# Perceiver block: x1 projected raw with column-centred weights, the inverse deviation applied afterwards

## What is computed

```
x = x + xattn(ctx, layernorm(x))          # scores, softmax over the 128 queries, context-weighted sum
x = x + attn(layernorm(x), w_attn, ...)   # 16 heads of 16, causal, T = 128
x = x + ffn(layernorm(x), W, b, V_r, C)   # W plus a rank-32 correction
layernorm(x) = (x - mean) / sqrt(var + 1e-5)
```

## Time and profile before

| what | value |
|---|---|
| median of 3 runs | 105.95 us (105.73 to 106.05) |
| the profiled execution | 105.76 us, of which the span of the instructions is 103.7 us |
| PE busy | 98.3 us of 103.7 |
| DVE, ACT, POOL busy | 76.3, 72.7, 63.8 us |
| read from memory | 27.59 MB |
| context loop, last weighing matmul | starts at 83.79 us |

### The profile page before, as it was taken

The page is one execution under the profiler, slowest core; times in us unless marked ns, Lnnn a source line. Parts: engine busy times, 40 slices in busy tenths (PEclk is TensorE's granted clock), DMA queues, the critical chain, the costliest instruction groups (busy, mean ns, idle before and its releaser), DMA issues.

```text
span 103.7 us, 2257 instructions
## 1 busy us (share of the span) xinstructions
PE 98.3 (95%) x740; PEld 86.4 (83%) x740; DVE 76.3 (74%) x217; ACT 72.7 (70%) x268; POOL 63.8 (62%) x46
## 2 busy tenths in 40 slices
PE   5999999999999999999999999999999999969990
PEld 1389999999999999999999999999998976845660
DVE  0412959959999999988777797777889745699641
ACT  4019599599999999997777977778879304489410
POOL 6405499869999999999766797666886001004020
PEclk9999999999999999999999999999999999999999
DMA  3899999999999999999999999993000000000001
GB/s 70 330 417 412 411 411 406 408 408 408 414 400 409 403 416 406 408 409 409 408 406 406 411 408 409 388 369 125 0 0 6 0 0 0 0 0 0 6 0 51
DMA packets 8746, 27.86 MB, mean 269 GB/s; under 512 B 1120, under 2 KB 1824, under 8 KB 8736
## 3 DMA queue, kind: packets, MB, share of 16 engines
q1 hardware_dynamic: 8736, 27.73, 68.3%
HBM read 27.59 MB, written 0.13 MB: 267 GB/s over the span
## 4 chain that ended last, share of the span: by engine, by line
PE 89%; DVE 4%; DMA 2%; issue 1%; POOL 1%; ACT 0%; DVEq 0%
PE bank L323 43%; PE bank L335 21%; PE bank L338 10%; DVE head_max L716 2%; DMA x<-x_dram 2%; PE bank L406 2%; PE bank L443 1%; PE bank L344 1%; PE bank L419 1%; PE bank L500 1%; PE bank L308 1%; PE bank L486 1%; PE bank L389 1%; PE bank L386 1%; PE bank L462 1%
## 5 line engine op out<-in xcount | busy, mean ns | idle before, releaser
L288 POOL TENSOR_TENSOR rows_split<-rows_ring,rows_split 128x1024 fp32r<-128x1024 f32 (+1 forms) x25 | 58.4, 2335 | 16.9 <-ACT rows_split L518 16.8
L323 PE MATMUL bank<-query_t,cols_ring 128*128 128x128 f32 x392 | 47.5, 276 | 0.0
L323 PEld LDWEIGHTS bank<-query_t,cols_ring 128*128 128x128 f32 x392 | 45.7, 192 | 1.3 <-ACT query_t L509 0.3
L529 ACT ACTIVATE bank<-bank,neg_max 128x128 f32<-128x128 f32 x98 | 33.1, 338 | 7.4 <-DVE neg_max L653 7.2
L335 PE MATMUL bank<-rows_split,probs 128*128 128x512 f32 x92 | 34.7, 413 | 0.0
L518 ACT CAST rows_split<-rows_ring 128x1024 fp32r<-128x1024 f32 (+1 forms) x25 | 25.8, 1033 | 6.1 <-DMA rows_ring<-ctx_rows_dram 5.1
L670 DVE SCALAR_TENSOR_TENSOR probs<-bank,inv_sums,probs 128x128 fp32r<-128x128 f32 x98 | 27.6, 345 | 0.9
L338 PE MATMUL bank<-rows_split,probs 128*128 128x256 f32 x92 | 25.6, 279 | 0.0
L653 DVE TENSOR_REDUCE neg_max<-bank 128x4 f32<-128x512 f32 (+1 forms) x25 | 16.8, 672 | 8.6 <-PE bank L323 8.6
L335 PEld LDWEIGHTS bank<-rows_split,probs 128*128 128x128 f32 x92 | 17.3, 189 | 3.1
L529 ACT ACTIVATION_READ_ACCUMULATOR bank<-bank,neg_max 128x1 f32 x98 | 19.8, 202 | 0.0
(11 more groups left out here) (96 smaller groups left out, 64.0 us busy)
## 6 DMA issues: line engine op xcount, KB each, us to landing
cols_ring<-ctx_cols_dram SPq DMA_DIRECT2D x24, 512.0 KB, 14.8
rows_ring<-ctx_rows_dram SPq DMA_DIRECT2D x24, 512.0 KB, 15.2
wqk_sb<-w_qk_dram SPq DMA_DIRECT2D x1, 512.0 KB, 11.6
cols_ring<-ctx_cols_dram SPq DMA_DIRECT2D x1, 256.0 KB, 11.3
rows_ring<-ctx_rows_dram SPq DMA_DIRECT2D x1, 256.0 KB, 12.1
wv_sb<-w_v_dram SPq DMA_DIRECT2D x1, 256.0 KB, 11.7
wproj_sb<-w_proj_dram SPq DMA_DIRECT2D x1, 256.0 KB, 10.4
wffn_sb<-w_ffn_dram SPq DMA_DIRECT2D x1, 256.0 KB, 9.7
```

The source lines that it names most:

```text
L288: pool.tensor_tensor(rows_split[:, b, 0:n, 1, :], rows_ring[:, slot * STEP:slot * STEP + n, :], rows_split[:, b, 0:n, 0, :].bitcast(F32), ...
L323: last = pe.matmul(into[:, t * P:(t + 1) * P], cols_ring[:, slot * STEP + t, c, :], query_t[:, c, :], start=(c == 0), stop=(c == DC - 1))
L529: last = act.activation(on[:, t * P:(t + 1) * P], on[:, t * P:(t + 1) * P], ACT.Exp, bias=neg_max[:, b, t:t + 1], accum_out=sums[:, b, t:t ...
```

## The change

1. A third copy of the q, k and v weights, turned (`w_t`, 768 KB), is loaded. Its load and those of `w_qk` (512 KB) and `w_v` (256 KB) are issued in the context loop, behind the rows of three steps (`WT_AT` = 13: in the iterations s = 13, 15, 17).
2. DVE sums it along its free axis in three parts at the ends of its steps 14, 15 and 16, and scales the 128 x 6 sums to negative means at its step 17.
3. SP stores those 768 means to memory, element by element (4 bytes each), behind the loads of the last rows; waits until they have landed; loads them back broadcast to all partitions (384 KB); and then issues the eight other weight loads.
4. POOL adds the means to the weights in six parts of 128 x 256: two in its loop behind the row splits of steps 20 and 21, four behind the loop.
5. x1 is turned raw and projected; DVE multiplies the identity by rstd, PE spreads that over all partitions with a matrix of ones, ACT copies the raw projections, DVE multiplies each by the spread rstd, and ACT, POOL and DVE add biases. The values take rstd in `scalar_tensor_tensor`, four instructions in place of two.
6. x1_bias moves from DVE to POOL. The rank-32 correction is no longer summed with the feed-forward weight on PE but by POOL (128 x 512).

```diff
+                if s == WT_AT:
+                    sp.dma_start(wt_sb[:], w_t).then_inc(wt_landed, 16)
+                if s == WT_AT + 2:
+                    sp.dma_start(wqk_sb[:], w_qk).then_inc(wqkv_landed, 16)
+                if s == WT_AT + 4:
+                    sp.dma_start(wv_sb[:], w_v).then_inc(wqkv_landed, 16)
             load_rows(STEPS - 2)
             load_rows(STEPS - 1)
+            sp.wait_ge(neg_means_ready, 1)
+            sp.dma_start(col_means.rearrange("o (n p) -> p (o n)", p=P), neg_means[:],
+                         allow_slow_non_contiguous=True).then_inc(means_stored, 16)
+            sp.wait_ge(means_stored, 16)
+            sp.dma_start(means_wide[:].rearrange("p n d -> p (n d)"), col_means.to_broadcast([P, 3 * D]))\
+              .then_inc(means_landed, 16)
             for dst, src in weights:
...
+            def centre_weights(n):
+                pool.wait_ge(means_landed, 16)
+                pool.wait_ge(wqkv_landed, 32)
...
+                pool.tensor_tensor(part, part, means_wide[:, n, :].unsqueeze(1).to_broadcast([P, DC, P]),
+                                   ALU.add).then_inc(wqkv_centred, 1)
...
+                if CENTRE_AT <= s < CENTRE_AT + DC:
+                    centre_weights(s - CENTRE_AT)
+            for n in range(DC, 3 * DC):
+                centre_weights(n)
...
-            turn_normed(1)
-            mask_scores(1)
+            for c in range(DC):
+                pe.wait_ge(x1_ready, c + 1)
+                pe.transpose(turn[c][:, 0:P], x1[:, c * P:(c + 1) * P], ident[:]).then_inc(turned, 1)
+            pe.wait_ge(wqkv_centred, 3 * DC)
...
                 if n == 1:
-                    pe.wait_ge(wffn_ready, 1)
+                    pe.wait_ge(diag_ready, 1)
+                    pe.wait_ge(ones_ready, 1)
+                    pe.wait_ge(raw_copied, 1)
+                    pe.matmul(rstd_wide_ps, ones[:], rstd_diag[:], start=True, stop=True).then_inc(rstd_spread, 1)
...
+            for c in range(DC):
+                act.wait_ge(k_ready, c + 1)
+                act.copy(raw[:, DC + c, :], k_ps[c][:, 0:P]).then_inc(raw_copied, 1)
+                act.wait_ge(q_ready, c + 1)
+                act.copy(raw[:, c, :], q_ps[c][:, 0:P]).then_inc(raw_copied, 1)
...
+            for i, n in enumerate([DC, 0, DC + 1, 1]):
+                dve.wait_ge(raw_copied, i + 1)
+                dve.tensor_tensor(scaled[:, n, :], raw[:, n, :], rstd_wide_ps, ALU.mult).then_inc(scaled_ready, 1)
```

More of the change, by code:

```diff
@@ L104, in perceiver_kernel @@
         ct_sb = sb("ct_sb", [R, D])
+        wt_sb = sb("wt_sb", [P, 3 * DC, D])
+        col_sums = sb("col_sums", [P, 3 * DC])
+        neg_means = sb("neg_means", [P, 3 * DC])
+        means_wide = sb("means_wide", [P, 3 * DC, P])
+        ones = sb("ones", [P, P])
+        rstd_diag = sb("rstd_diag", [P, P])
+        raw = sb("raw", [P, 2 * DC, P])
+        scaled = sb("scaled", [P, 2 * DC, P])
+        bk_parity = sb("bk_parity", [P, DC, 2])
+        low_rank = sb("low_rank", [P, DC * D])
         q_t = sb("q_t", [P, DC, P])
@@ L204, in perceiver_kernel @@
         out_stored = sem("out_stored")
-        weights = [(wqk_sb, w_qk), (bqk_sb, b_qk), (wv_sb, w_v), (bv_sb, b_v.to_broadcast([P, D])),
+        weights = [(bqk_sb, b_qk), (bv_sb, b_v.to_broadcast([P, D])),
                    (wproj_sb, w_proj), (bproj_sb, b_proj.to_broadcast([P, D])), (wffn_sb, w_ffn), (bffn_sb, b_ffn.to_broadcast([P, D])),
@@ L562, in _ @@
                .then_inc(x1_bias_centred_ready, 1)
[L564 to L568, removed]
             def exps_by_head(j):
@@ L612, in link, with statistics @@
                 dve.wait_ge(dve_step, link_count[0])
-            def layer_norm(n, src):
+            def statistics(src):
                 link(dve.bn_stats(bn[:, 0:6], src))
                 dve.bn_aggr(mean_var[:], bn[:]).then_inc(stats_ready, 1)
[L617 to L629, removed]
             dve.memset(warm[:], 0.0).then_inc(warm_ready, 1)
+            dve.memset(ones[:], 1.0).then_inc(ones_ready, 1)
             dve.memset(bn[:, 6:8], 0.0).then_inc(eps_ready, 1)
@@ L636, in _ @@
             dve.wait_ge(x_landed, 16)
-            layer_norm(0, x0[:])
-            copy_turn(0, query_t)
+            statistics(x0[:])
+            dve.wait_ge(stats_ready, 1)
+            dve.wait_ge(rstd_ready, 1)
+            for c in range(DC):
+                half = slice(c * P, (c + 1) * P)
+                dve.tensor_scalar(normed[:, half], x0[:, half], mean_var[:, 0:1], rstd[:, 0:1],
+                                  ALU.subtract, ALU.mult).then_inc(normed_ready, 1)
+            dve.wait_ge(turned, DC)
+            dve.tensor_copy(query_t[:, 1, :], turn[1][:, 0:P]).then_inc(turn_copied, 1)
             def invert(s):
@@ L673, in normalize, with sum_columns @@
                 last.then_inc(probs_ready, 1)
+            def sum_columns(third):
+                dve.wait_ge(wt_landed, 16)
+                part = slice(third * DC, (third + 1) * DC)
+                dve.tensor_reduce(col_sums[:, part], wt_sb[:, part, :], AX_X, ALU.add).then_inc(sums_ready, 1)
             for s in range(STEPS + 1):
@@ L692, in _ @@
             dve.wait_ge(summed, STEPS)
[L693 to L698, removed]
-            for c in range(DC):
[L700 to L704, removed]
+            for c in range(DC):
+                half = slice(c * P, (c + 1) * P)
+                dve.tensor_tensor(x1[:, half], weighted_end[:, half], x0[:, half], ALU.add).then_inc(x1_ready, 1)
+            dve.wait_ge(x1_ready, DC)
+            statistics(x1[:])
+            dve.wait_ge(rstd_ready, 2)
+            dve.tensor_scalar(rstd_diag[:], ident[:], rstd[:, 0:1], None, ALU.mult).then_inc(diag_ready, 1)
+            dve.wait_ge(rstd_spread, 1)
+            for i, n in enumerate([DC, 0, DC + 1, 1]):
+                dve.wait_ge(raw_copied, i + 1)
+                dve.tensor_tensor(scaled[:, n, :], raw[:, n, :], rstd_wide_ps, ALU.mult).then_inc(scaled_ready, 1)
+            dve.wait_ge(scaled_ready, 2 * DC)
+            dve.wait_ge(bq_scaled_ready, 1)
+            dve.tensor_scalar(q_t[:, 1, :], scaled[:, 1, :], SCALE, bq_scaled[:, 1:2], ALU.mult, ALU.add)\
+               .then_inc(q_copied[1], 1)
             def copy_exp_t(j):
@@ L740, in _ @@
             for e in range(2):
-                dve.tensor_tensor(v_pad[:, :, e, :, e * HD:(e + 1) * HD], v_view[:, :, e], bv_view[:, :, e],
-                                  ALU.add).then_inc(v_copied, 1)
+                for c in range(DC):
+                    dve.scalar_tensor_tensor(v_pad[:, c, e, :, e * HD:(e + 1) * HD], v_view[:, c, e], rstd[:, 0:1],
+                                             bv_view[:, c, e], ALU.mult, ALU.add).then_inc(v_copied, 1)
             copy_exp_t(0)
```

81 lines of the change are left out of this document (65 added, 16 removed).

## The result

| | median | runs |
|---|---|---|
| before | 105.84 us | 6 (105.65 to 106.23) |
| changed | 113.89 us | 6 (113.51 to 114.66) |

The ratio is 1.076 (95% interval 1.073 to 1.080). The forecast was 109.8 us, range 107.5 to 112.3: right in sign and place, and only half of the size. The profiled execution has a span of 112.2 us.

The account below looks back on a forecast made before the run. PE was taken as the bound (busy 98.3 of 103.7 us), beside a full memory pipe. Late means +2.4, head scores +1.4 and values' bias +0.3 made +4.1 on 105.76: 109.9, rounded down to 109.8 us, range 107.5 to 112.3.

Parts of the forecast that it names:

- Full pipe, no overtaking: Memory at 409 GB/s in the loop: the store of the means waits behind the last rows, landing at 71.1 us.
- When the means land: Store of the means done at 73.5 us, broadcast load 2.2 plus 0.64 us: means land at 76.4 (74.9 to 78.1).
- the lower bound: Cheapest price of the store of the means: 19 ns per piece and engine, 0.9 us for 48 pieces.
- The Trainium skill's rule: A transfer costs about 2.0 us plus bytes at 436 GB/s, many descriptors little extra: means near 76.0 us.
- POOL's chain: After the means: 10.1 us to the last split, loop ends 3.3 us late; 13.1 to centred weights; projections +2.4 us.
- projections ended by POOL's last part: Expected sign in the trace: PE waits at the projections for POOL's last centring part, near 89.6 us.
- Projections to head scores, +1.4: From the projections' start to the last head score: 4.8 us instead of 3.3, costing +1.4 us (+1.0 to +1.9).
- Values' bias, +0.3: Four half-size instructions instead of two for the values' bias: between nothing and 0.48 us more, taken as +0.3 us.
- What was costed at nothing: Loads in the loop (1.57 MB, 3.84 us lateness), DVE's three sums, x1_bias and feed-forward sum on POOL: no cost.
- Rival A: Store not queued behind the context, means back by about 64 us, kernel not slower: 105.5 to 106.2 us; 15%.
- Rival B: Scattered 4-byte store dearer, 150 ns a piece, 7.2 us: means land at 81.2, about 114.6 us; 8%.
- Rival C: The 1.57 MB loaded in the loop starve ACT of rows, up to 3.84 us on PE, time near 110; 5%.

Follow-up runs that it names:

- the low-rank edit alone: Kernel before the change, with only the feed-forward weight's addition to the rank-32 correction moved from PE (L389) to POOL: 107.48 us, ratio 1.014.

## Why the prediction was wrong

- **Full pipe, no overtaking:** right. The store, ready at 61, could not land before about 71. Traffic fell between 69 and 71 us, forecast 71.
- **"When the means land":** this step failed, in both of its terms. The store was priced by its pieces, 19 to 85 ns each, from the landing of bqk_sb, a load. The pieces themselves were cheap: packets were over before 72, under 1 us behind the last packets of the rows, at the lower bound. What I left out was that the landing of a store in such pieces can come long after its last packet; it was stored at 76.5, outside even my upper bound (71.1 + 4.1 = 75.2). The runs give 4 us to the placing of the pieces. The store was 3.0 us later than forecast; the load was sized at 2.84 and measured 4.8. Together 5.0 us, against a miss of 4.1 in the time; in part that is because the chain behind the means was 0.6 us shorter than forecast.
- **The Trainium skill's rule** weighed there ("DMA: Bandwidth & Descriptors", "Anatomy of one DMA — SWDGE (gpsimd) path") is given there for transfers issued from GpSimd, and these came from SP. It was right that many descriptors come at little extra (about 0.5 us for 640 more), and its 2.0 us of fixed cost, mostly the receipt of the write, named the kind of term I lacked; here over 4 us were measured between last packet and landing, and its 76.0 us for the means is 5.4 under the measured 81.4.
- **POOL's chain:** right. Forecast 10.1 us from means to the last split and 13.1 to the last part, measured 9.6 and 12.4. The projections started 12.6 us behind the means, forecast 13.2. But the sign "projections ended by POOL's last part" did not show: I had let the turn of x1 start as soon as x1 was there, and left out that the rank-32 products (L448, 1.12 us) stand ahead of it on PE. That way ended with ACT's copies at 94.0, POOL's last part at 93.75, so the omission changed the number by no more than 0.2 us.
- **Projections to head scores, +1.4:** right, 4.7 us from 93.97 to 98.70, forecast 4.8.
- **Values' bias, +0.3:** right, 0.85 instead of 0.48 us.
- **What was costed at nothing** (loads in the loop, sums, x1_bias and the sum on POOL): right, shown by the run without the round trip, 105.95 us. DVE's sums took 0.68 us each, and in the changed kernel PE was busy for all of the 74 us from 5 to 79.
- **Rival A** gave 105.5 to 106.2 us for means that come in time; three runs in that state measured 105.95, 105.73 and, reordered, 105.61. Its mechanism, a store served beside the rows, fell with ACT's queue. **Rival B** (the store dearer than the bqk row suggests) is what happened, by another cause than the price of a piece. I gave it 8%, and its 114.6 us were nearer than the forecast. **Rival C** did not show.

Of the 8.0 us, 4.1 go with the placing of the stored pieces alone (113.89 to 109.75, of which 0.4 is the faster load behind them), some 0.7 more with rows of 24 bytes (109.0), and 3.3 with the place of the centring parts (to 105.73).

## What to carry to other kernels

A small store on a critical path is priced by when it lands, not by its packets: write it in whole rows, or at least try another spacing (a gap of one element was worth 4 us here), and look in the trace for silence between last packet and landing. A wait put into an engine's program costs what is queued behind it, so put the work that needs a late transfer behind the work that does not. And before removing "useless" matmuls, look at what they keep running: the idle time that this opened on PE was dearer here than the work.

## What had not been expected of the hardware

- 768 pieces of 4 bytes landed over 4 us behind their last packet where they lay side by side in memory, and under 1.1 us behind it with a gap of one element between neighbours (last packets after 71.5 us, stored at 72.5).
- A transfer issued just ahead suffers too: the last rows landed 17.7 us after issue in the change, 13.2 with rows of 24 bytes and 14.1 without the round trip.
- With the low-rank edit alone, 1.19 us of PE idle time were followed by a granted clock of 0.55 for 3.3 us, though PE had been busy for 80 us. In the changed kernel 5.4 us of idle time were followed by 0.50 (1.2 GHz) for 3 us, which cost little there because POOL was the bound.
- Idle time does not always bring the clock down. With the pieces spaced by partition, PE stood for 3.20 us and then worked with gaps, and the windows from 80 and 83 us (columns as above) have the full clock. What decides between the two is not shown.

```profile
82.29 0.50 PE L403 MATMUL bank<-rows_split,probs 128*128 128x512 f32 x1 [3.20 <-POOL rows_split L339]
...
80.00:83.00 3.00, 0.71 (x4) 0.62 (x5) 1.23 (x6) 0.97 (x4) 3.00 (x3) 1.00 0.33 106
83.00:86.00 3.00, 1.64 (x10) 1.19 (x9) 0.00 (x0) 1.16 (x4) 3.00 (x2) 1.00 0.00 0
```
